# Attention side jobs of a gated cross-attention block cut into smaller steps

## The chip, the cores and the metric

One core of a Trainium2 chip runs the whole program: TensorE (matmul), VectorE, ScalarE, GpSimd and SyncE, with 16 DMA engines. The metric is device time in microseconds of one execution; lower is better.

## What is computed

The reference, cut to what matters:

```python
def xattn(f, txt):                       # f = layernorm(x): 2 x 2048 rows of 512; txt: 2 x 77 x 512
    txt_proj = txt @ Ws
    feat_proj = f @ W
    h = tanh(txt_proj[:, None] + feat_proj[:, :, None] + b)    # 2 x 2048 x 77 x 512
    rho = einsum('bftd,d->bft', h, w) + (1 - q_mask) * NEG
    att = softmax(rho, axis=-1)
    txt_h = att @ txt
    return tanh(txt_h @ Wcw + bcw) * f + tanh(txt_h @ Wcb + bcb)

def ffn(x):                              # 512 -> 1408 -> 512
    xq = fake_quant(layernorm(x))        # rounded to 127 levels of its largest magnitude
    h = fake_quant(silu(xq @ q(w_gate).T) * (xq @ q(w_up).T))
    return h @ q(w_down).T               # q: each weight row rounded to 127 levels

x = x + tanh(g_xattn) * xattn(layernorm(x), ctx)
x = x + tanh(g_ffn) * ffn(x)
```

## The kernel before

The attention is a pipeline over 924 *pieces*. A piece is one text token t and one block e of 128 features: its columns are rows of x. Pieces 0 to 307 (stage 0, 4 x 77) take the 2048 rows of batch 0, 308 to 615 (stage 1, from `PER_B`) the first 1536 rows of batch 1, 616 to 923 (stage 2, from `LAST`) its last 512. For each piece VectorE adds a column of `atxt` to the projected features `feat` and writes the sum into a ring (`add_text`, line 681); ScalarE takes the tanh in place (line 491); TensorE multiplies by the vector w and collects the scores in PSUM (`score`, line 1024, in stage 2 line 1029). ScalarE works on *units* of 6144 columns: 3 pieces in stage 0 (numbered 0 to 102), 4 in stage 1, 12 in stage 2. The ring has room for three units, so VectorE may write a piece only when TensorE has scored the one whose place it takes (`free_at`): about 9 pieces back in stage 0, 12 in stage 1, 36 in stage 2.

Each engine runs through the pieces in a loop of its own in program order, and dictionaries from piece number to job hang *side jobs* into the loops, ahead of that piece's own work. The order within a piece is that of the loop's `if`s. The names end in `_AT`; `later(at)` is `at + 10` up to piece 295 and `at + 13` after it, the piece at which VectorE fetches what TensorE made at `at`. The side jobs:

- *Projections* (`FEATS`, `FEAT_AT`, `project`, line 971): 32 blocks of 128 features by 512 rows, four matmuls each into a PSUM bank; the first four are made ahead of the loop. Phase ph (77 pieces) needs the blocks of its own e; `turns` lists at which piece of the phase before TensorE makes them. VectorE copies each block to `feat` (`copy_feat`, line 581).
- *Rows of batch 1*: statistics (`STATS_AT`, line 616), a chain of 18 small instructions (`CHAIN_AT`), then for 16 tiles normalise (`NORM_AT`, line 624), row maximum (`MAX1_AT`, line 629), transposes on TensorE (line 961), and `copy_xnT` (`COPY_AT`, line 687), which overwrites the rows of batch 0 in `xnT` and therefore waits with `dve.wait_ge(projected, Q4 * EC)` (line 686) for all 16 projections of batch 0. `MAX0_AT` holds the row maxima of batch 0.
- *Weight blocks* (`JOBS`, `QUANT_AT`): 15 blocks of the feed-forward weights (11 of 1024 columns, 4 of 1408), each reduced, scaled and rounded by VectorE (`quantise_weights`, lines 764 to 779), transposed by TensorE (`WT_AT`, line 1058) and copied out (`WCOPY_AT`). SyncE loads the next block when one is rounded.
- *Softmax*: scores are fetched (`RHO_AT`), transposed in four parts (`TSCORE_AT`, line 1042), shifted by their maximum (`SHIFT_AT`, lines 707 and 709), exponentiated by ScalarE (`EXP_AFTER`) and summed (`SUMS_AT`, `soft_sums`, lines 718 to 727).

The feed-forward part follows after the attention.

Of the kernel before, what the change touches and what calls it, by code (L numbers as in the profile page):

```python
# [5 lines left out]
def flamingo_gated_block(nc, x, ctx_in, q_mask, g_xattn, g_ffn, Ws, W, w, b, Wcw, bcw, Wcb, bcb,  # L6
# [44 lines left out]
    Q4 = 4  # L51
# [9 lines left out]
    with stack:  # L61
# [106 lines left out]
        TB, FB, WB, AB, SOFTB = (3, 4), (5, 6), (7, 4), (2, 7, 7, 7), (3, 4, 5, 6)  # L168
# [103 lines left out]
        MAX0_AT = {12 + 2 * i: i for i in range(BT)}  # L272
# [4 lines left out]
        CHAIN_AT = 150  # L277
        NORM_AT = {172 + 7 * i: i for i in range(BT)}
# [4 lines left out]
        for ph in range(B * EC):  # L283
            turns = {3: (2, 4, 14, 16), 4: (14, 16, 30, 58), 5: (30, 32, 46, 48)}.get(ph, (24, 26, 38, 40))
            for part in range(Q4 if ph < EC + 2 else Q4 - 1):
                if ph:
                    FEAT_AT[(ph - 1) * T + turns[part]] = len(FEATS)
                FEATS.append((ph // EC, ph % EC, part, ph % 2, part * 512))
        for k in range(2):
            FEAT_AT[(B * EC - 1) * T + 24 + 2 * k] = len(FEATS)  # L290
            FEATS.append((1, 2 + k, Q4 - 1, 0, k * 512))
        LAST_FEAT = ((0, 3 * 512), (1, 3 * 512), (0, 0), (0, 512))
        FEAT_COPY_AT = {later(at): f for at, f in FEAT_AT.items()}
# [20 lines left out]
        MSTD_AT, SD_AT = 530, 545  # L314
# [8 lines left out]
        def _(sp):  # L323
# [26 lines left out]
            for p in range(PIECES):  # L350
                if p in STATS_AT:
                    i = STATS_AT[p]
                    sp.wait_ge(stats_ready, BT + i + 1)
                    x_again(i + 4)
                if p in MAX1_AT and MAX1_AT[p] + 4 < BT:
                    i = MAX1_AT[p]
                    sp.wait_ge(max_ready, i + 1)
                    sp.wait_ge(xn_transposed, BT + i + 1)
                    x_again(i + 4)
                if p in QUANT_AT and QUANT_AT[p] + 1 < NJOB:  # L360
                    sp.wait_ge(wq_ready, QUANT_AT[p] + 1)
                    weight_in(QUANT_AT[p] + 1)

# [206 lines left out]
        def _(dve):  # L570
# [178 lines left out]
            def quantise_weights(job):  # L749
# [3 lines left out]
                step = width // parts  # L753
                whole = wstage[:, 0:width]
                dve.wait_ge(wt_in, sum(WT_BYTES[:job + 1]))

                def scaled():
                    for c in range(parts):
                        part = wstage[:, c * step:(c + 1) * step]
                        last = v.tensor_scalar(part, part, wsc[:, 2 + c:3 + c], MAGIC, ALU.mult, ALU.add)  # L760
                    return last

                for k, op in enumerate((
                        lambda: v.tensor_reduce(wsc[:, 0:parts], whole.rearrange("p (c d) -> p c d", c=parts), AX,  # L764
                                                ALU.max, apply_absolute_value=True),
                        lambda: v.tensor_scalar(wsc[:, 0:parts], wsc[:, 0:parts], 1.0 / QMAX, None, ALU.mult),
                        lambda: v.reciprocal(wsc[:, 2:2 + parts], wsc[:, 0:parts]),
                        scaled)):
                    if k:
                        dve.wait_ge(wt_step, lead + k)  # L770
                    op().then_inc(wt_step, 1)
                dve.wait_ge(wt_step, lead + 4)
                if job:
                    dve.wait_ge(wq_transposed, job)
                v.tensor_scalar(wq_sb[:, 0:width], whole, MAGIC, QMAX, ALU.subtract, ALU.min).then_inc(wq_ready, 1)
                if kind == "d":
                    move(sd[:, row:row + 1], wsc[:, 0:1])
                else:
                    move(sgu[:, row, :], wsc[:, 0:2])
# [12 lines left out]
            for p in range(EARLY, PIECES):  # L792
# [16 lines left out]
                if p == CHAIN_AT:  # L809
                    block_stats(BT, BT, 3)  # L810
# [9 lines left out]
                if p in FEAT_COPY_AT:  # L820
                    copy_feat(FEAT_COPY_AT[p])
                if p in WCOPY_AT:
                    copy_weights(WCOPY_AT[p])
                if p in QUANT_AT:
                    quantise_weights(QUANT_AT[p])
# [127 lines left out]
        def _(pe):  # L953
# [10 lines left out]
            def project(n):  # L964

                bt, e, part, _, _ = FEATS[n]
                pe.wait_ge(xnT_ready, BT * bt + 4 * (part + 1))
                if n >= 2:
                    pe.wait_ge(feat_ready, n - 1)
                for k in range(EC):  # L970
                    last = mm(bank(FB[n % 2]), w_sb[:, k, e * P:(e + 1) * P], xnT[:, k, part * 512:(part + 1) * 512],  # L971
                              start=(k == 0), stop=(k == EC - 1))
                last.then_inc(projected, 1)
# [72 lines left out]
            def transpose_weights(job):  # L1046
                kind, _ = JOBS[job]
                pe.wait_ge(wq_ready, job + 1)
                if job:
                    pe.wait_ge(wq_copied, job)  # L1050
                else:
                    pe.wait_ge(atxt_ready, EC)
# [4 lines left out]
                for bk, col, src in chunks:  # L1057
                    last = nc.tensor.transpose(bankb(WB[bk])[:, col:col + P], wq_sb[:, src:src + P], identb[:, :])
                last.then_inc(wq_transposed, 1)

            for p in range(PIECES):
# [17 lines left out]
                if p in FEAT_AT:  # L1079
                    n = FEAT_AT[p]  # L1080
                    if FEATS[n][:3] == (1, 1, 0):
                        pe.wait_ge(shifted, Q4)
                    project(n)
                if p in WT_AT:
                    transpose_weights(WT_AT[p])
# [114 lines left out]
```

## Time and profile before

| | us |
|---|---|
| median of 3 runs | 1412.11 |
| lowest, highest | 1405.0, 1412.8 |
| the profiled execution, its own time | 1408.1 |
| span of its profile, first to last instruction | 1406.3 |

| engine | busy us | share of the span |
|---|---|---|
| TensorE, matmul | 1110.7 | 79% |
| VectorE | 1168.8 | 83% |
| ScalarE | 1260.0 | 90% |
| GpSimd | 13.9 | 1% |

The pieces run from about 50 to 1140 us. In the rows, PE is TensorE, PEld its weight loads, DVE VectorE, ACT ScalarE; L491 is line 491. An entry in brackets is idle time of the engine ahead of that row, and who ended it. Matmuls of fp32 appear as two records each, and four column groups of scoring run side by side.

### The profile page before, as it was taken

The page shows a single profiled execution, that of the slowest core. Times are in us where ns is not written, and L with a number is a line of the kernel's source. Part 1 is how long each engine was busy: PE and PEld are TensorE (multiplying, and loading weights), DVE is VectorE, ACT ScalarE, POOL GpSimd, SP SyncE. Part 2 cuts the span into 40 slices and gives each one's busy share as a digit, 9 for nine tenths or more (in the row PEclk, how much of TensorE's full clock was granted, in tenths as well). Part 3 has the DMA queues.
Part 4 walks back from the last instruction along what each step waited for, and adds up shares of the span by engine and source line. Part 5 has one row for each costly group of instructions (what it writes and reads, how often), then busy time and mean ns, then how long its engine had stood idle before and what let it go on. Part 6 is the DMA issues. An engine that isn't in the chain of part 4 may idle for free.

```text
span 1406.3 us, 16785 instructions
## 1 busy us (share of the span) xinstructions
PE 1110.7 (79%) x6891; PEld 369.2 (26%) x6891; DVE 1168.8 (83%) x1679; ACT 1260.0 (90%) x481; POOL 13.9 (1%) x32
## 2 busy tenths in 40 slices
PE   6887768778767776679779779787667659999898
PEld 4322112212212221123222122121111115444343
DVE  7688898887899898788978878868899947888777
ACT  3998999899999999999999999999999966666695
POOL 3000000000000000000000000000000000000000
PEclk9998889889998998999999999999998879999999
DMA  6000011100010000000000010000000004411196
GB/s 219 1 15 16 16 45 60 53 23 1 23 38 32 22 24 0 1 1 6 31 21 6 16 43 1 1 0 0 1 1 0 1 16 142 150 52 48 64 346 211
DMA packets 29872, 61.43 MB, mean 44 GB/s; under 512 B 3771, under 2 KB 5835, under 8 KB 29797
## 3 DMA queue, kind: packets, MB, share of 16 engines
q1 hardware_dynamic: 27840, 59.52, 12.7%
q8 instruction: 54, 0.88, 0.3%
q10 hardware_dynamic: 1253, 0.85, 0.2%
q14 instruction: 21, 0.17, 0.0%
q0 software_dynamic: 704, 0.01, 0.0%
HBM read 46.20 MB, written 14.16 MB: 43 GB/s over the span
## 4 chain that ended last, share of the span: by engine, by line
ACT 59%; PE 27%; DVE 13%; issue 1%; DMA 0%; SPq 0%; DVEq 0%
ACT big L491 58%; PE ps L1151 10%; DVE big L681 8%; PE ps L1169 6%; PE ps L971 5%; PE ps L1024 3%; PE ps L1029 1%; DVE bn L616 1%; PE ps L1117 1%; PE ps L1131 0%; DMA wgu<-in_x_dram 0%; DVE big L581 0%; DVE wsc L764 0%; DVE wgu L624 0%; PE ps L961 0%
## 5 line engine op out<-in xcount | busy, mean ns | idle before, releaser
L491 ACT ACTIVATE big<-big 128x6144 f32<-128x6144 f32 (+2 forms) x205 | 1063.6, 5279 | 21.4 <-DVE big L681 21.3
L681 DVE TENSOR_SCALAR big<-big,atxt 128x2048 f32<-128x2048 f32 (+2 forms) x918 | 792.8, 922 | 154.6 <-PE ps L1024 139.5
L1024 PE MATMUL ps<-big,wslide 128*32 128x512 f32 x4312 | 615.1, 643 | 215.3 <-ACT big L491 212.0
L1024 PEld LDWEIGHTS ps<-big,wslide 128*32 128x32 f32 x4312 | 143.3, 114 | 645.0 <-ACT big L491 335.4
L1151 PE MATMUL ps<-aux,wgu 128*128 128x512 bf16 x680 | 151.5, 379 | 0.0
L1029 PE MATMUL ps<-big,wslide 128*32 128x512 f32 x616 | 91.1, 700 | 43.4 <-ACT big L491 43.4
L971 PE MATMUL ps<-big,aux 128*128 128x512 f32 x256 | 118.3, 605 | 2.1 <-ACT big L449 2.1
L536 ACT ACTIVATE aux<-ps,sgux 128x512 f32<-128x512 f32 x88 | 59.9, 686 | 56.8 <-PE ps L1151 55.9
L916 DVE SCALAR_TENSOR_TENSOR big<-ps,sgux,aux 128x512 f32<-128x512 f32 x88 | 65.9, 749 | 25.3 <-PE ps L1151 17.0
L1151 PEld LDWEIGHTS ps<-aux,wgu 128*128 128x128 bf16 x680 | 65.3, 98 | 73.4
L1169 PE MATMUL ps<-wd,wgu 128*128 128x512 bf16 x352 | 78.1, 386 | 3.0 <-DVE wgu L932 3.0
L971 PEld LDWEIGHTS ps<-big,aux 128*128 128x128 f32 x256 | 46.2, 190 | 73.1 <-issue 69.4
L919 DVE TENSOR_REDUCE hm<-big 128x1 f32<-128x512 f32 x88 | 60.4, 686 | 3.0
L1029 PEld LDWEIGHTS ps<-big,wslide 128*32 128x32 f32 x616 | 21.3, 123 | 109.4 <-ACT big L491 63.2
L549 ACT ACTIVATE big<-big,gmax 128x1408 int16<-128x1408 f32 x32 | 46.1, 1453 | 3.5 <-DVE gmax L882 3.5
L1169 PEld LDWEIGHTS ps<-wd,wgu 128*128 128x128 bf16 x352 | 34.8, 99 | 46.0 <-issue 5.7
L946 DVE TENSOR_TENSOR aux<-ps,aux 128x512 f32<-128x512 f32 x32 | 21.9, 685 | 16.7 <-DMA out_dram<-aux 8.9
L511 ACT ACTIVATE aux<-aux,beta,alpha 128x512 int16<-128x512 f32 x32 | 25.8, 809 | 9.4 <-DVE sgux L891 5.2
L557 ACT ACTIVATE aux<-aux,resB,resA 128x512 f32<-128x512 f32 x32 | 25.7, 802 | 6.1 <-DVE aux L949 4.6
L449 ACT ACTIVATE big<-ps 128x512 f32<-128x512 f32 x16 | 8.9, 596 | 17.2 <-PE ps L961 17.2
L949 DVE TENSOR_TENSOR aux<-aux 128x512 f32<-128x512 f32 x32 | 22.1, 692 | 1.1
L519 ACT ACTIVATE aux<-ps 128x512 bf16<-128x512 bf16 x32 | 18.9, 591 | 4.1 <-PE ps L1117 4.1
(153 smaller groups left out, 419.3 us busy)
## 6 DMA issues: line engine op xcount, KB each, us to landing
aux<-in_x_dram SPq DMA_DIRECT2D x96, 256.0 KB, 2.7
out_dram<-aux SPq DMA_DIRECT2D x32, 256.0 KB, 3.6
hidden_spill<-big SPq DMA_DIRECT2D x6, 768.0 KB, 5.5
big<-hidden_spill SPq DMA_DIRECT2D x6, 768.0 KB, 7.3
wgu<-in_x_dram SPq DMA_DIRECT2D x11, 256.0 KB, 7.3
aux<-in_L_ffn_w_gate_dram SPq DMA_DIRECT2D x11, 256.0 KB, 2.6
aux<-in_L_ffn_w_up_dram SPq DMA_DIRECT2D x11, 256.0 KB, 2.9
aux<-in_L_ffn_w_down_dram SPq DMA_DIRECT2D x4, 704.0 KB, 4.0
```

Source lines behind the costliest of these rows:

```text
L491: nc.scalar.activation(unit, unit, ACT.Tanh).then_inc(tanh_done, 1)
L511: nc.scalar.activation(xu[:, n % 2, :], xt[:, n % 3, :], ACT.Identity, bias=beta[:, n:n + 1], scale=alpha[:, n:n + 1]).then_inc(xu_ready, 1)
L536: nc.scalar.activation(sg[:, m % 2, :], bank(m % 3), ACT.Silu, scale=sgux[:, i, 0:1])\
L549: nc.scalar.activation(h_int[:, slot2[q], :, j, 0:P], part, ACT.Copy, scale=gmax[:, 3:4]).then_inc(hu_ready, 1)
L681: v.tensor_scalar(ring[:, place(p)], src, atxt[:, e, bt * T + t:bt * T + t + 1], None, ALU.add).then_inc(sums_ready, 1)
L916: v.scalar_tensor_tensor(h_slots[:, rb % SLOTS, i, :], bank(3 + m % 3), sgux[:, i, 1:2], sg[:, m % 2, :], ALU.mult, ALU.mult).then_inc(h_r ...
L919: v.tensor_reduce(hm[:, m:m + 1], h_slots[:, rb % SLOTS, i, :], AX, ALU.max, apply_absolute_value=True).then_inc(dve_step, 1)
L971: last = mm(bank(FB[n % 2]), w_sb[:, k, e * P:(e + 1) * P], xnT[:, k, part * 512:(part + 1) * 512], start=(k == 0), stop=(k == EC - 1))
L1024: last = mm(bank(k)[32 * part:32 * part + 32, :], wslide[:, e, 31 - g:63 - g], unit[:, part * 512:(part + 1) * 512], start=(e == 0 and g = ...
L1029: last = mm(bank(LB)[32 * j:32 * j + 32, :], wslide[:, e, 31 - g:63 - g], unit, start=(e == 0 and g == 0), stop=True, skip_group_check=True)
L1151: last = mm(bank(3 * g + m % 3), wgu8[:, 2 * k + g, i * P:(i + 1) * P], xqT[:, rb % 2, k, :], start=(k == 0), stop=(k == EC - 1))
L1169: last = mm(bank(n % 6), hq[:, q % 2, i, j * P:(j + 1) * P], wd[:, i, :], start=(i == 0), stop=(i == IC - 1))
```

## The change

Projections become four single matmuls, at the piece given by `turns` and two, four and six pieces later, and `turns` itself is set anew; TensorE's waits stand at the first, the signal at the last. Weight blocks become four steps of VectorE in successive pieces, at new pieces (`JOB_AT`), and their transposes two halves. The chain of 18 becomes three parts of six. The rows of batch 1 start at piece 164, every 6 pieces, instead of 172, every 7; row maxima of batch 0 stand every 4 pieces instead of 2. Score transposes, shifts and sums are spread wider, the sums of batch 0 ten pieces apart instead of four, and the score transposes use banks 3 and 4 only, so parts 2 and 3 wait for parts 0 and 1 to be shifted. Two waits of VectorE on its own earlier work are added: at the start of a chain, and ahead of the first copy of a phase's features.

```diff
-        TB, FB, WB, AB, SOFTB = (3, 4), (5, 6), (7, 4), (2, 7, 7, 7), (3, 4, 5, 6)
+        TB, FB, WB, AB, SOFTB = (3, 4), (5, 6), (7, 4), (2, 7, 7, 7), (3, 4, 3, 4)
...
-        MAX0_AT = {12 + 2 * i: i for i in range(BT)}
+        MAX0_AT = {12 + 4 * i: i for i in range(BT)}
...
-        CHAIN_AT = 150
-        NORM_AT = {172 + 7 * i: i for i in range(BT)}
+        CHAIN_AT = {148 + 2 * k: k for k in range(3)}
+        NORM_AT = {164 + 6 * i: i for i in range(BT)}
         MAX1_AT = {at + 2: i for at, i in NORM_AT.items()}
         COPY_AT = {later(at): i for at, i in NORM_AT.items()}
...
-            turns = {3: (2, 4, 14, 16), 4: (14, 16, 30, 58), 5: (30, 32, 46, 48)}.get(ph, (24, 26, 38, 40))
+            turns = {3: (-17, -9, 2, 10), 5: (20, 30, 40, 50)}.get(ph, (10, 20, 30, 40))
             for part in range(Q4 if ph < EC + 2 else Q4 - 1):
                 if ph:
-                    FEAT_AT[(ph - 1) * T + turns[part]] = len(FEATS)
+                    for k in range(EC):
+                        FEAT_AT[(ph - 1) * T + turns[part] + 2 * k] = len(FEATS), k
...
-            FEAT_AT[(B * EC - 1) * T + 24 + 2 * k] = len(FEATS)
+            for i in range(EC):
+                FEAT_AT[(B * EC - 1) * T + 10 + 12 * k + 2 * i] = len(FEATS), i
...
-        FEAT_COPY_AT = {later(at): f for at, f in FEAT_AT.items()}
+        FEAT_COPY_AT = {max(later(at), T * (FEATS[f][1] - 1)): f
+                        for at, (f, k) in FEAT_AT.items() if k == EC - 1}
...
-        QUANT_AT = dict(zip((50, 64, 80, 96, 112, 128, 200, 220, 262, 365, 378, 400, 445, 475, 522), range(NJOB)))
-        WT_AT = {at + 1: j for at, j in QUANT_AT.items()}
-        WCOPY_AT = {later(at + 1): j for at, j in QUANT_AT.items()}
+        JOB_AT = (59, 75, 91, 107, 123, 179, 204, 229, 262, 276, 290, 400, 430, 460, 490)
+        QUANT_AT = {at + k: (job, k) for job, at in enumerate(JOB_AT) for k in range(4)}
+        WT_AT = {at + 4 + h: (job, h) for job, at in enumerate(JOB_AT) for h in range(2)}
+        WCOPY_AT = {later(at + 5): job for job, at in enumerate(JOB_AT)}
...
-        TSCORE_AT = {PER_B + 1 + c: (0, c) for c in range(Q4)}
-        TSCORE_AT.update({LAST + 42 + 2 * c: (1, c) for c in range(Q4)})
-        SHIFT_AT = {PER_B + 16 + 4 * c: (0, c) for c in range(Q4)}
-        SHIFT_AT.update({LAST + 84 + 24 * c: (1, c) for c in range(Q4)})
-        EXP_AFTER = {UNIT_OF[at] + 2: f for at, f in SHIFT_AT.items()}
-        SUMS_AT = {at + (24 if at < LAST else 72): f for at, f in SHIFT_AT.items()}
+        TSCORE_AT = {PER_B + at: (0, c) for c, at in enumerate((3, 6, 34, 40))}
+        TSCORE_AT.update({LAST + at: (1, c) for c, at in enumerate((42, 48, 100, 112))})
+        SHIFT_AT = {PER_B + at: (0, c) for c, at in enumerate((20, 26, 48, 54))}
+        SHIFT_AT.update({LAST + at: (1, c) for c, at in enumerate((84, 96, 140, 152))})
+        EXP_AFTER = {UNIT_OF[at] + 1: f for at, f in SHIFT_AT.items()}
+        SUMS_AT = {PER_B + at: (0, c) for c, at in enumerate((62, 72, 82, 92))}
+        SUMS_AT.update({LAST + at: (1, c) for c, at in enumerate((180, 204, 228, 252))})
...
-        MSTD_AT, SD_AT = 530, 545
+        MSTD_AT, SD_AT = 520, 530
...
-                if p in QUANT_AT and QUANT_AT[p] + 1 < NJOB:
-                    sp.wait_ge(wq_ready, QUANT_AT[p] + 1)
-                    weight_in(QUANT_AT[p] + 1)
+                if p in QUANT_AT and QUANT_AT[p][1] == 3 and QUANT_AT[p][0] + 1 < NJOB:
+                    sp.wait_ge(wq_ready, QUANT_AT[p][0] + 1)
+                    weight_in(QUANT_AT[p][0] + 1)
...
-                    if k:
+                    if lead + k:
                         dve.wait_ge(dve_chain, lead + k)
...
-                if p == CHAIN_AT:
-                    block_stats(BT, BT, 3)
+                if p in CHAIN_AT:
+                    k = CHAIN_AT[p]
+                    dve.wait_ge(stats_ready, TILES)
+                    chained(STAT * 3 + 6 * k, mean_rstd_ops(slice(BT, TILES))[6 * k:6 * k + 6])
...
                 if p in FEAT_COPY_AT:
+                    if FEATS[FEAT_COPY_AT[p]][2] == 0 and p > T:
+                        dve.wait_ge(sums_ready, T * (p // T) - EARLY)
                     copy_feat(FEAT_COPY_AT[p])
...
-            def project(n):
+            def project(n, steps=range(EC)):
...
-                pe.wait_ge(xnT_ready, BT * bt + 4 * (part + 1))
-                if n >= 2:
-                    pe.wait_ge(feat_ready, n - 1)
-                for k in range(EC):
+                if 0 in steps:
+                    pe.wait_ge(xnT_ready, BT * bt + 4 * (part + 1))
+                    if n >= 2:
+                        pe.wait_ge(feat_ready, n - 1)
+                for k in steps:
...
-                last.then_inc(projected, 1)
+                if EC - 1 in steps:
+                    last.then_inc(projected, 1)
...
             def transpose_scores(bt, c):
+                if c >= 2:
+                    pe.wait_ge(shifted, Q4 * bt + c - 1)
```

Left out here are the body of `quantise_weights`, which does the same instructions in steps 0 (reduction), 1 (scale and reciprocal), 2 (scaling) and 3 (rounding, signal), and that of `transpose_weights`, cut into the first four chunks and the rest. A wait of TensorE for `shifted`, ahead of the first projection of phase 5, falls away with the new banks.

## Rows read from the trace of the kernel before

**Rows 1.** The page, part 1: busy us, share of the span, instructions.

```profile
PE 1110.7 (79%) x6891; PEld 369.2 (26%) x6891; DVE 1168.8 (83%) x1679; ACT 1260.0 (90%) x481; POOL 13.9 (1%) x32
```

**Rows 2.** Waits, whole span: who waited for whom, us, times, longest us.

```profile
PE ps L1024 <- ACT big L491: 212.0, 130, 6.3
DVE big L681 <- PE ps L1024: 139.5, 119, 3.6
ACT big L491 <- DVE big L681: 21.3, 15, 4.5
```

**Rows 3.** Waits from 53 to 330, to 600, to 690, to 1023, to 1141 us.

```profile
ACT big L491 <- DVE big L681: 11.0, 5, 4.5
...
ACT big L491 <- DVE big L681: 1.3, 1, 1.3
...
ACT big L491 <- DVE big L681: 3.6, 3, 2.2
...
ACT big L491 <- DVE big L681: 3.7, 3, 1.9
...
ACT big L491 <- DVE big L681: 1.8, 3, 0.8
```

**Rows 4.** Chain that ended last, two stretches: start us, us, what.

```profile
116.01 3.75 PE ps L971 x8
...
121.61 3.63 PE ps L971 x8
...
128.19 1.14 DVE wsc L764
...
132.67 94.00 ACT big L491 x18
...
638.92 1.85 PE ps L1024 x12
```

**Rows 5.** Timeline, ScalarE, TensorE, VectorE in stage 0: start us, us, what, idle before.

```profile
273.26 234.79 ACT L491 ACTIVATE big<-big 128x6144 f32<-128x6144 f32 x45 [3.79 <-DVE big L681]
...
325.58 2.78 PE L1024 MATMUL ps<-big,wslide 128*32 128x512 f32 x24 [0.73 <-ACT big L491]
...
326.71 3.68 DVE L681 TENSOR_SCALAR big<-big,atxt 128x2048 f32<-128x2048 f32 x3 [0.51 <-PE ps L1024]
...
349.16 1.13 PE L971 MATMUL ps<-big,aux 128*128 128x512 f32 x2
...
440.31 3.52 PE L1024 MATMUL ps<-big,wslide 128*32 128x512 f32 x16 [2.44 <-ACT big L491]
443.76 0.70 PE L961 MATMUL ps<-ident,aux 128*128 128x128 f32 x4
```

**Rows 6.** Timeline, VectorE: row jobs of stage 0, a sum and a weight block.

```profile
453.94 0.54 DVE L624 TENSOR_SCALAR aux<-aux,mean,rstd 128x512 f32<-128x512 f32 x1
...
458.59 0.68 DVE L687 COPY big<-ps 128x512 f32<-128x512 f32 x1
...
649.77 0.95 DVE L718 TENSOR_TENSOR aux<-big,crow 128x768 f32<-128x768 f32 x1
...
652.16 3.80 DVE L681 TENSOR_SCALAR big<-big,atxt 128x1536 f32<-128x1536 f32 x4
...
662.91 1.21 DVE L764 TENSOR_REDUCE wsc<-aux 128x2 f32<-128x1024 f32 x1
...
666.15 1.94 DVE L681 TENSOR_SCALAR big<-big,atxt 128x1536 f32<-128x1536 f32 x2
```

**Rows 7.** Windows: us, busy by engine, granted clock of PE, DMA share, GB/s.

```profile
140.00:310.00 170.00, 126.01 (x844) 32.74 (x840) 148.89 (x173) 165.27 (x33) 0.00 (x0) 0.87 0.13 41
680.00:1013.00 333.00, 260.25 (x1633) 70.89 (x1633) 272.38 (x340) 329.32 (x65) 0.00 (x0) 1.00 0.03 12
```

**Rows 8.** Timeline, VectorE in stage 2: a sum and 24 additions.

```profile
1086.86 0.75 DVE L718 TENSOR_TENSOR aux<-big,crow 128x576 f32<-128x576 f32 x1
...
1088.75 9.58 DVE L681 TENSOR_SCALAR big<-big,atxt 128x512 f32<-128x512 f32 x24
```

More of the change, by code:

```diff
@@ L747, in soft_last, with quantise_weights @@
                 v.tensor_reduce(num[:, :, TILES - Q4:TILES], prod_last, AX, ALU.add).then_inc(soft_step, 1)
-            def quantise_weights(job):
+            def quantise_weights(job, step):
                 kind, row = JOBS[job]
@@ L752, in quantise_weights @@
                 lead = 4 * job
-                step = width // parts
+                part = width // parts
                 whole = wstage[:, 0:width]
-                dve.wait_ge(wt_in, sum(WT_BYTES[:job + 1]))
-                def scaled():
-                    for c in range(parts):
[L759 to L777, printed above, removed]
-                else:
-                    move(sgu[:, row, :], wsc[:, 0:2])
+                if step == 0:
+                    dve.wait_ge(wt_in, sum(WT_BYTES[:job + 1]))
+                    v.tensor_reduce(wsc[:, 0:parts], whole.rearrange("p (c d) -> p c d", c=parts), AX,
+                                    ALU.max, apply_absolute_value=True).then_inc(wt_step, 1)
+                elif step == 1:
+                    dve.wait_ge(wt_step, lead + 1)
+                    v.tensor_scalar(wsc[:, 0:parts], wsc[:, 0:parts], 1.0 / QMAX, None, ALU.mult).then_inc(wt_step, 1)
+                    dve.wait_ge(wt_step, lead + 2)
+                    v.reciprocal(wsc[:, 2:2 + parts], wsc[:, 0:parts]).then_inc(wt_step, 1)
+                elif step == 2:
+                    dve.wait_ge(wt_step, lead + 3)
+                    for c in range(parts):
+                        row_part = wstage[:, c * part:(c + 1) * part]
+                        last = v.tensor_scalar(row_part, row_part, wsc[:, 2 + c:3 + c], MAGIC, ALU.mult, ALU.add)
+                    last.then_inc(wt_step, 1)
+                else:
+                    dve.wait_ge(wt_step, lead + 4)
+                    if job:
+                        dve.wait_ge(wq_transposed, job)
+                    v.tensor_scalar(wq_sb[:, 0:width], whole, MAGIC, QMAX, ALU.subtract, ALU.min).then_inc(wq_ready, 1)
+                    if kind == "d":
+                        move(sd[:, row:row + 1], wsc[:, 0:1])
+                    else:
+                        move(sgu[:, row, :], wsc[:, 0:2])
@@ L824, in _ @@
                 if p in QUANT_AT:
-                    quantise_weights(QUANT_AT[p])
+                    quantise_weights(*QUANT_AT[p])
                 if p in RHO_AT:
@@ L962, in transpose_rows @@
                 last.then_inc(xn_transposed, 1)
-            def project(n):
+            def project(n, steps=range(EC)):
                 bt, e, part, _, _ = FEATS[n]
-                pe.wait_ge(xnT_ready, BT * bt + 4 * (part + 1))
-                if n >= 2:
-                    pe.wait_ge(feat_ready, n - 1)
-                for k in range(EC):
+                if 0 in steps:
[3 more added lines that the diff above has]
+                for k in steps:
                     last = mm(bank(FB[n % 2]), w_sb[:, k, e * P:(e + 1) * P], xnT[:, k, part * 512:(part + 1) * 512],
-                              start=(k == 0), stop=(k == EC - 1))
-                last.then_inc(projected, 1)
+                              start=(k == 0), stop=(k == EC - 1), skip_group_check=True)
+                if EC - 1 in steps:
+                    last.then_inc(projected, 1)
             def project_text(e):
@@ L1044, in transpose_scores, with transpose_weights @@
                 last.then_inc(rho_transposed, 1)
-            def transpose_weights(job):
+            def transpose_weights(job, half):
                 kind, _ = JOBS[job]
[L1048 to L1052, printed above, removed]
+                if half == 0:
+                    pe.wait_ge(wq_ready, job + 1)
+                    if job:
+                        pe.wait_ge(wq_copied, job)
+                    else:
+                        pe.wait_ge(atxt_ready, EC)
                 if kind == "d":
@@ L1056, in transpose_weights @@
                     chunks = [(0, (2 * k + g) * P, g * D + k * P) for k in range(EC) for g in range(2)]
-                for bk, col, src in chunks:
+                for bk, col, src in chunks[4:] if half else chunks[:4]:
                     last = nc.tensor.transpose(bankb(WB[bk])[:, col:col + P], wq_sb[:, src:src + P], identb[:, :])
-                last.then_inc(wq_transposed, 1)
+                if half:
+                    last.then_inc(wq_transposed, 1)
             for p in range(PIECES):
@@ L1079, in _ @@
                 if p in FEAT_AT:
[L1080 to L1083, printed above, removed]
+                    n, k = FEAT_AT[p]
+                    project(n, (k,))
                 if p in WT_AT:
-                    transpose_weights(WT_AT[p])
+                    transpose_weights(*WT_AT[p])
                 if p == SD_AT + 1:
```

## The prediction

> **What bounds the kernel now.** I read the page's engine line first, then the waits, the chain, and the timeline around the longest waits. ScalarE is the busiest engine, 1260.0 us of the 1406.3 [rows 1]. In the attention it does little but the tanh over units of 6144 columns; 45 of them in a row took 234.79 us, 5.22 us each [rows 5]. The first question is therefore how long ScalarE waits there: 21.3 us, in 15 waits, every time for VectorE's additions (line 681) [rows 2]. That is all a rearrangement of side jobs can give back. The same waits by stretch show where: 11.0 us up to 330, 1.3 up to 600, 3.6 around 650, 3.7 up to 1023 and 1.8 after it [rows 3].
>
> The chain tells why. Before the longest wait (4.5 us [rows 2], ending at 132.67 [rows 4]) TensorE runs two whole projections, 3.75 and 3.63 us, with two pieces between them; scoring is late, VectorE gets its ring slots late, then meets a weight block at 128.19, and ScalarE runs dry [rows 4]. A weight block holds VectorE from 662.91 to 666.15, 3.24 us; a softmax sum from 649.77 to 652.16, 2.4 us [rows 6].
>
> How much lateness is free? In a clean stretch TensorE starts scoring a unit at 325.58; VectorE follows with three additions from 326.71 and is done at 330.39, 4.8 us after 325.58 [rows 5]. Those additions are read two tanhs after that scoring starts, 10.4 us. So up to about 5.6 us of lateness costs nothing, and what is over is ScalarE's wait. Per piece VectorE has free time of 5.22/3 - 1.2 = 0.54 us in stage 0 (three additions in 3.68 us less the overlap [rows 5]) and 5.22/4 - 0.93 = 0.37 in stage 1 (four in 3.80 [rows 6]). As a test: from piece 348 to 365 the old schedule has sums at 348, 352, 356 and 360, copies at 351, 353 and a weight block at 365: with the copies 4 x 2.4 + 1.3 + 3.2 = 14.1 us against 17 x 0.37 = 6.3 free, 7.8 over; less 5.6 leaves 2.2, and the two projections at 354 and 356 make it worse; the trace has 3.6 [rows 3]. The rule is good to a microsecond or so.
>
> **The change, part by part.**
>
> *Projections.* 28 blocks of 3.63 us become 112 single matmuls, one every second piece. What does a single one cost TensorE? A quarter of 3.63 is 0.91, the lower bound, if coming and going between line 1024 and line 971 costs nothing. A row that ends after the first matmul of a projection (two records of line 971) has 1.13 for it [rows 5], the upper bound, with its own start and end. I take 1.1, as each now stands alone. In stage 0 a unit then has 2.78 us of scoring [rows 5] plus at most 2 x 1.1: 5.0, under 5.22. In stage 1 ten pieces have 10 x 0.92 (two pieces 1.85 [rows 4]) + 4 x 1.1 = 13.6 against 10 x 1.305 = 13.05: 0.55 late for each projection, some 2 us over the four from piece 328 on, and with the score transposes in the same stretch about 3 to 4. That stays inside 5.6. So the projections' waits go.
>
> The Trainium skill (TensorEngine Tiling (Array Packing), Overview, Key Properties) speaks against this part: changing the tiling mode, not just the tile, drains TensorE. Scoring runs on 128*32 and the projection on 128*128, so the changes of mode rise from 56 to 224. The trace agrees in kind: 1.13 for one against 0.91 for a quarter of four [rows 4, 5]. The page has no price for it; with the drain at 1.13 as without it at 0.91 the sum is the same, as both stay inside the free lateness, and only far more would move it (second rival).
>
> *Softmax.* The sums stand ten pieces apart instead of four: 2.4 against 10 x 0.37 = 3.7 free. The 3.6 us around 650 go. At piece 400 the last sum meets the first step of a weight block of 1408 columns: 2.4 + at most 4.5 (3.24 x 1408/1024) in four pieces, 3.7 of additions: 10.6 us where 5.2 + 5.6 = 10.8 are to be had. It just fits; I put 0.3 there.
>
> *Weight blocks in steps and the statistics chain in three.* The same instructions, so VectorE's sum is unchanged; each dip is shared among four pieces. The new waits of VectorE on its own earlier instruction (chain start, the part-0 copies) have what they wait for many pieces behind them, but at piece 154, where it is the instruction before: nothing to 0.2 us. SyncE issues the next block's two loads at the fourth step instead of the only one, 11 or more pieces (19 us) ahead of their use, behind waits that VectorE meets in the same order: hidden.
>
> *Stage 2.* VectorE needs 9.58 us for 24 additions [rows 8] where ScalarE has 10.44: 0.45 us free per unit. A sum takes 1.9 [rows 8]. Before, shifts and sums from 700 to 844 (4 x 1.9, and 4 x 0.9, estimated as half a sum, 11 us) ran against some 12 units x 0.45; now to 868, with the score transposes on TensorE set apart. I count the 1.8 us [rows 3] as gone, with nothing to 1.8 as bounds.
>
> *A new wait.* The second batch's rows move from piece 172 on to 164 on, and the copy that overwrites xnT with the first of them from 182 to 174. That copy waits for all 16 projections of batch 0 (line 686). The last is still not done before piece 170 on TensorE. VectorE can run some 9 pieces ahead of TensorE's scoring in stage 0; 182 was 12 pieces behind 170 and never met that wait, 174 is 4 behind and must. Everything queued behind it on VectorE waits too, the additions first. Let E be the end of tanh for pieces 168-170. TensorE then scores 168 and 169 (2 x 0.93), transposes rows at 170 (0.70 [rows 5]) and does the last matmul (1.1): E + 3.65. VectorE: copy 0.6 (0.68 with its overlap), additions 174 and 175 of 1.2 each, normalise 0.5 [rows 6], addition 176 of 1.28: E + 8.4. ScalarE, done with 171-173, wants it at E + 5.2: 3.2 us idle. The lead is now zero, so what comes next costs in full: pieces 177-179 with a row maximum 0.6 and the weight block's 1.2 reduction make 5.4 against 5.2, idle 0.2; 180-182 with two copies (1.2), the other 2.0 of the block, a normalise 0.5 and 3.6 of additions make 7.3, idle 2.1. Together 5.5 us. From below: 3 us if the block is better hidden than that; from above 8.5 if TensorE is at its lower clock then, since two pieces there took 3.52 instead of 1.85 [rows 5] and a matmul stretches alike.
>
> *Sum.* 21.3 - 5.5 - 0.3 - 0.4 for small dips = 15.1 us. The profiled execution took 1408.1, so 1393.0. The three timed runs have a median of 1412.1, 0.3% above that execution; the same 15.1 from it gives **1397 us**, a ratio of 0.989.
>
> **Rivals.**
>
> *All of it comes back.* The wait at 174 finds VectorE late anyway, or TensorE earlier than I reckon. For it: VectorE waited 139.5 us for scoring in all, and little of that reached ScalarE [rows 2]. Against it: TensorE's order at 170 is fixed. Then 21.3 - 0.5: 1412.1 - 20.8 = 1391.
>
> *TensorE cannot carry the single matmuls in stage 1, and the wait at 174 is dearer.* At 1.5 us each, ten pieces need 15.2 against 13.05, 2.1 late per projection: the four from 328 make 8.6 and are 3 over the 5.6; the others of stage 1 stand in groups of two or three and stay near it. With 8.5 at 174: 21.3 - 8.5 - 3 - 1 = 9, 1403. For it: 1.13 is one row, and no row has a lone matmul between scorings. Against: TensorE waited 212.0 us for ScalarE [rows 2], and 84 more comings and goings at 0.2 are 17.
>
> *Slower: TensorE's clock.* With its bursts of two projections gone, TensorE might stay at 1.2 GHz for long. At that level two pieces took 3.52 [rows 5], 5.3 a unit, just over a tanh, before any side job. From 140 to 310 the granted clock is 0.87, so about a quarter of that time is already at the lower level, and the slow scoring at 440.31 came after TensorE had waited 2.44 us for ScalarE [rows 5]; from 680 to 1013 it is 1.00 [rows 7]. If it stayed low through stage 0's 103 units, scoring (5.3) and the 64 single matmuls there at 2.2 (1.4 a unit) would make 6.7 a unit against 5.2: 103 x 1.5 = 155 us more. It decides from 29 us of that, about a fifth: 15 for the gain and 14 beyond, 1426 and up. Against it: single matmuls stand in the gaps after which the clock fell.
>
> The Trainium skill (TensorE: Matmul & The Clock Gate, section HAM oscillation) sides with this rival: short bursts with idle between them let the clock drop again and again, and it advises doing the matmuls in one go ahead of a wait. Here two in one go preceded ScalarE's longest wait [rows 4]; what the rule would do is in the 155 us above.
>
> **How the numbers follow.** The forecast (12 to 19 us gained) 0.48; all back 0.15; half lost (4 to 12 gained) 0.31; slower 0.06. A measurement of this kernel can tell about 1% from no change, 14.1 us. Faster by over 1%: the second, 0.15, and some 0.34 of the first, as 14.1 lies a third of the way up its 12 to 19: 0.49. Within 1%: 0.14 + 0.31 = 0.45. Slower 0.06. The range reaches from 1388, all back in a run of the faster kind, to 1408, where 4 us are gained; the forecast alone is 1393 to 1400.
>
> **What would show it.** Right: ScalarE's waits for line 681 fall from 21.3 to 5-8 us, and the longest are two or three close together near 340 us, behind a VectorE copy of line 687's kind that waits for TensorE's projection; no wait remains near 130, 270, 660 and 745; line 971 costs TensorE about 1.1 per matmul. Wrong: waits between 630 and 760 with TensorE never idle (second rival), a granted clock well under 0.87 between 140 and 310 (third), or no long VectorE wait near 340 (first).

## The result, and the profile after

The changed kernel's median is 1389.0 us (1387.7 to 1392.0), against 1409.6 for the kernel before (four runs of each): a ratio of 0.9875, 95% interval 0.9853 to 0.9897. That is 20.6 us faster, where 15 were forecast; the time lies inside the range, close to its lower end. It is 8 us under the 1397 of the forecast: 5.5 of them are the larger gain, and 2.5 the kernel before, whose median was 1412.1 in three runs and is 1409.6 in four.

| | before | after |
|---|---|---|
| profiled execution, us | 1408.1 | 1387.7 |
| its span | 1406.3 | 1385.9 |
| ScalarE's waits for the additions | 21.3 in 15 | 5.0 in 3 |

The page, part 1, of the changed kernel (busy us, share of the span, instructions; compare [rows 1]):

```profile
PE 1114.8 (80%) x6868; PEld 348.3 (25%) x6891; DVE 1167.7 (84%) x1679; ACT 1258.5 (91%) x481; POOL 13.9 (1%) x32
```

VectorE and ScalarE work as long as before to 0.2%, and TensorE's matmuls a little longer; only the span is shorter. In the changed kernel line 681 is 687 (additions), 491 is 497 (tanh), 1024 is 1035 (scoring), 971 is 981 (projection), 686 and 687 are 692 and 693 (copy to `xnT`). Its waits, whole span (us, times, longest; compare [rows 2]):

```profile
PE ps L1035 <- ACT big L497: 186.9, 137, 5.6
...
DVE big L687 <- PE ps L1035: 117.0, 145, 2.7
...
DVE big L693 <- PE ps L981: 7.9, 1, 7.9
...
ACT big L497 <- DVE big L687: 5.0, 3, 3.1
```

The third line is new: one copy of VectorE that waits 7.9 us for a projection. The timeline of ScalarE shows what is left of its waits (start us, us, what, idle before; compare [rows 3, 5]):

```profile
51.46 292.14 ACT L497 ACTIVATE big<-big 128x6144 f32<-128x6144 f32 x56
346.68 10.63 ACT L497 ACTIVATE big<-big 128x6144 f32<-128x6144 f32 x2 [3.09 <-DVE big L687]
358.95 259.19 ACT L497 ACTIVATE big<-big 128x6144 f32<-128x6144 f32 x50 [1.64 <-DVE big L687]
...
1096.12 24.57 ACT L497 ACTIVATE big<-big 128x6144 f32<-128x6144 f32 x6 [0.26 <-DVE big L687]
1124.57 0.47 ACT L501 ACTIVATE big<-big 128x320 f32<-128x320 f32 x1 [3.88 <-DVE big L743]
```

Fifty-six tanhs run without a gap from 51.46, where the old kernel had waits up to 4.5 us; then come two waits, 3.09 and 1.64, and one of 0.26 in stage 2. VectorE's timeline around the two:

```profile
332.73 1.28 DVE L687 TENSOR_SCALAR big<-big,atxt 128x2048 f32<-128x2048 f32 x1
341.91 0.69 DVE L693 COPY big<-ps 128x512 f32<-128x512 f32 x1 [7.90 <-PE ps L981]
342.52 2.47 DVE L687 TENSOR_SCALAR big<-big,atxt 128x2048 f32<-128x2048 f32 x2
344.91 0.55 DVE L630 TENSOR_SCALAR aux<-aux,mean,rstd 128x512 f32<-128x512 f32 x1
345.37 2.48 DVE L687 TENSOR_SCALAR big<-big,atxt 128x2048 f32<-128x2048 f32 x2
...
349.55 1.21 DVE L763 TENSOR_REDUCE wsc<-aux 128x2 f32<-128x1024 f32 x1
```

The copy stands at piece 174, the two additions are 174 and 175, normalise and addition 176 follow, and 346.68 is when ScalarE gets them. TensorE's timeline has the other side, the last matmul of projection 15 at piece 170, behind the transposes of a row tile:

```profile
338.44 1.92 PE L1035 MATMUL ps<-big,wslide 128*32 128x512 f32 x16 [0.18 <-ACT big L497]
340.29 0.66 PE L970 MATMUL ps<-ident,aux 128*128 128x128 f32 x4
340.78 1.02 PE L981 MATMUL ps<-big,aux 128*128 128x512 f32 x2
```

From 338.44 the forecast counted 3.65 us to the end of that matmul; the copy starts 3.47 after it.

Where do the 20.4 us of span come from? From the start of the first tanh to the end of the last one it is 1069.2 us instead of 1087.1, 17.9 less. ScalarE's waits give 16.3 of that. Each wait also costs the overlap of two tanhs: 45 in a row run 5.22 us apart [rows 5] while one alone lasts 5.33 (the row at 549.57 further down is such a one); twelve waits fewer are some 1.2 us. Outside that stretch, the first tanh starts at 51.46 instead of 52.85 (1.4), the last exponential waits 3.88 instead of 5.41 (1.5), and 0.4 are lost after it. That 1.4 and 1.5 are the change's is not shown: among the nine experiments below, the first tanh starts between 51.6 and 56.2, and the last wait is 3.9 in three and 5.3 to 5.4 in six, where kernels that are alike at that end have either value. It goes with the length of the last 40 records of scoring on TensorE: 4.66 us in the four traces with the short wait, 6.1 to 6.2 in the other seven. The granted clock in them is 1.00 here and 0.72 before (windows of those records).

### The profile page after: what moved, and what is told of

Its sections match the earlier page's. It is cut to its first block, busy times and chain, and to the rows that moved or that the text cites. A ratio compares the mean times of both kernels' runs of the same rounds, so it can differ in the third digit from the quotient of the medians.

```text
span 1385.9 us, 16773 instructions
## 1 busy us (share of the span) xinstructions
PE 1114.8 (80%) x6868; PEld 348.3 (25%) x6891; DVE 1167.7 (84%) x1679; ACT 1258.5 (91%) x481; POOL 13.9 (1%) x32
## 4 chain that ended last, share of the span: by engine, by line
ACT 72%; PE 19%; DVE 8%; issue 1%; DMA 0%; SPq 0%; DVEq 0%
ACT big L497 71%; PE ps L1164 11%; PE ps L1182 6%; DVE big L687 4%; DVE bn L622 1%; PE ps L981 1%; PE ps L1130 1%; PE ps L1144 0%; DMA wgu<-in_x_dram 0%; PE ps L1040 0%; DVE wgu L630 0%; ACT big L469 0%; ACT big L455 0%; DVE block_sums L730 0%; DVE aux L724 0%
## 5 line engine op out<-in xcount | busy, mean ns | idle before, releaser
L1035 PEld LDWEIGHTS ps<-big,wslide 128*32 128x32 f32 x4312 | 131.4, 112 | 611.4 <-ACT big L497 322.6
L981 PE MATMUL ps<-big,aux 128*128 128x512 f32 x256 | 140.3, 638 | 2.1 <-ACT big L455 2.1
L981 PEld LDWEIGHTS ps<-big,aux 128*128 128x128 f32 x256 | 39.1, 188 | 99.1 <-issue 95.4
L1040 PEld LDWEIGHTS ps<-big,wslide 128*32 128x32 f32 x616 | 20.0, 120 | 108.0 <-ACT big L497 65.9
```

The lines of the kernel that those rows point to most:

```text
L1035: last = mm(bank(k)[32 * part:32 * part + 32, :], wslide[:, e, 31 - g:63 - g], unit[:, part * 512:(part + 1) * 512], start=(e == 0 and g = ...
L1040: last = mm(bank(LB)[32 * j:32 * j + 32, :], wslide[:, e, 31 - g:63 - g], unit, start=(e == 0 and g == 0), stop=True, skip_group_check=True)
```

## Experiments

Theory: ScalarE waits only for lateness beyond VectorE's lead, the 5 to 6 us by which its additions are ready before ScalarE wants them. So the gain is owed to where the jobs stand, not to how small they are, and the 5 us left are the wait of piece 174. The rivals: the cutting itself brought the gain; the weight block at 179 causes the waits that are left. Ratios are to the kernel before, run on the same chip; intervals are 95%. Most of these intervals overlap one another, so the differences between the kernels rest on the waits in one trace of each and on the stretch from the first tanh's start to the last one's end there, which leaves out the scatter of the beginning and the end.

| kernel | median us | ratio | interval | ScalarE's waits, us | first to last tanh, us |
|---|---|---|---|---|---|
| before | 1409.6 | 1 | | 21.3 | 1087.1 |
| changed | 1389.0 | 0.9875 | 0.9853 to 0.9897 | 5.0 | 1069.2 |
| rows from 170 | 1384.5 | 0.9843 | 0.9816 to 0.9870 | none | 1063.8 |
| rows from 170, whole projections | 1386.5 | 0.9857 | 0.9825 to 0.9889 | 0.6 | 1065.4 |
| rows from 170, whole weight blocks | 1386.1 | 0.9849 | 0.9834 to 0.9863 | 1.4 | 1065.4 |
| rows from 170, close sums | 1384.9 | 0.9849 | 0.9815 to 0.9882 | 0.8 | 1065.1 |
| rows from 170, all three in one go | 1393.7 | 0.9893 | 0.9871 to 0.9915 | 6.9 | 1072.1 |
| changed, weight block 5 at 190 | 1386.8 | 0.9857 | 0.9820 to 0.9895 | 3.1 | 1067.1 |
| before, new places for projections alone | 1392.2 | 0.9892 | 0.9876 to 0.9908 | 5.3 | 1069.9 |
| before, cut projections alone | 1399.1 | 0.9932 | 0.9906 to 0.9957 | 13.2 | 1078.9 |
| rows from 170, a dose of lateness (one run) | 1384.5 | | | 0.3 | 1064.4 |

**Rows from piece 170.**

```diff
-        NORM_AT = {164 + 6 * i: i for i in range(BT)}
+        NORM_AT = {170 + 6 * i: i for i in range(BT)}
```

> The changed kernel with one edit: the rows of batch 1 start at piece 170 instead of 164, so the copy that waits for all 16 projections stands at piece 180, ten behind the last projection matmul at 170. Theory (the wait at 174 caused both waits of ScalarE, 3.09 and 1.64 us): both vanish, ScalarE's waits fall from 5.0 to under 1 us, time about 5 us below the changed kernel, ratio to the kernel before about 0.984. Rival (the weight block at 179 to 182 meeting the row jobs is the cause): a wait of 1.5 us or more stays within pieces 180 to 188, gain at most 3 us.

Measured: 1384.5 us, 4.5 less than the changed kernel's median; from the first tanh to the last it is 5.4 less. ScalarE's timeline has 108 tanhs without a gap, to the first exponential of the softmax, and VectorE's first copy to `xnT`, now at piece 180, waits for nothing:

```profile
53.96 561.69 ACT L497 ACTIVATE big<-big 128x6144 f32<-128x6144 f32 x108
```

```profile
347.42 0.68 DVE L693 COPY big<-ps 128x512 f32<-128x512 f32 x1
```

Both waits are gone with the weight block where it was, so it was the wait at 174. By its waits this kernel is better than the changed one; the intervals of their two ratios overlap.

**Weight block 5 at 190.**

```diff
-        JOB_AT = (59, 75, 91, 107, 123, 179, 204, 229, 262, 276, 290, 400, 430, 460, 490)
+        JOB_AT = (59, 75, 91, 107, 123, 190, 204, 229, 262, 276, 290, 400, 430, 460, 490)
```

> The changed kernel with the rows from 164 as it has them, but weight block 5 at pieces 190 to 193 instead of 179 to 182. Theory: the first wait (3.1 us at unit 58) stays, the second (1.64 us at unit 60) goes or falls under 0.4; 1.3 to 1.7 us gained on the changed kernel. Rival (the block is the cause of both): both go, 4.7 us.

The first wait stays to the hundredth, the second is gone; VectorE still waits 7.9 us at its copy (timeline of ScalarE, then the waits):

```profile
347.47 269.62 ACT L497 ACTIVATE big<-big 128x6144 f32<-128x6144 f32 x52 [3.09 <-DVE big L687]
```

```profile
DVE big L693 <- PE ps L981: 7.9, 1, 7.9
```

The wait at 174 takes the lead, and the block that stands next then costs ScalarE 1.64 us. The rival of the block falls.

**Whole projections, new places.** On the first experiment:

```diff
                     n, k = FEAT_AT[p]
-                    project(n, (k,))
+                    if k == EC - 1:
+                        project(n)
```

> The first experiment's kernel (rows from 170), but each projection is again four matmuls in one go, at the piece of its last single matmul; the pieces ten apart stay. Theory of free lateness (5.3 to 5.6 us; a block of 3.63 us makes TensorE that late once and it catches up before the next): ScalarE's waits stay under 1.5 us, time within 2 us of the first experiment. Rival (it is the cutting into single matmuls that removed the waits): the waits of the kernel before come back at the projections, 8 us or more.

Measured: 0.6 us of waits, all that its timeline of ScalarE has:

```profile
98.86 386.34 ACT L497 ACTIVATE big<-big 128x6144 f32<-128x6144 f32 x74 [0.25 <-DVE big L687]
485.36 129.04 ACT L497 ACTIVATE big<-big 128x6144 f32<-128x6144 f32 x25 [0.15 <-DVE big L687]
...
1092.35 24.57 ACT L497 ACTIVATE big<-big 128x6144 f32<-128x6144 f32 x6 [0.20 <-DVE big L687]
```

Its median is 2.0 us over the first experiment's; the last exponential's wait alone differs by 1.5 in the profiles (5.40 against 3.88), and it falls either way. At ten pieces apart the cutting is worth 0.6 us of waits.

**Whole weight blocks.** On the first experiment, all four steps at the block's first piece:

```diff
-                    quantise_weights(*QUANT_AT[p])
+                    if QUANT_AT[p][1] == 0:
+                        for step in range(4):
+                            quantise_weights(QUANT_AT[p][0], step)
```

> The first experiment's kernel (rows from 170), but each weight block is rounded in one go at its first piece, as before. Theory: a block of 3.2 to 4.4 us in one piece is inside the free lateness; the lead was least (0.13 us) at the block of pieces 430 to 433, so 0 to 2 us of ScalarE's waits in all. Rival (the steps removed waits): 3 us or more.

Measured: two waits, 1.03 at piece 430's block, as expected of the place with the least lead, and 0.36 in stage 2, where no weight block stands. Timelines of VectorE and ScalarE:

```profile
730.89 1.61 DVE L763 TENSOR_REDUCE wsc<-aux 128x1 f32<-128x1408 f32 x1
...
734.78 3.80 DVE L687 TENSOR_SCALAR big<-big,atxt 128x1536 f32<-128x1536 f32 x4
```

```profile
736.76 292.27 ACT L497 ACTIVATE big<-big 128x6144 f32<-128x6144 f32 x56 [1.03 <-DVE big L687]
```

**Close sums.** On the first experiment:

```diff
-        SUMS_AT = {PER_B + at: (0, c) for c, at in enumerate((62, 72, 82, 92))}
+        SUMS_AT = {PER_B + at: (0, c) for c, at in enumerate((62, 66, 70, 74))}
```

> The first experiment's kernel, but the four softmax sums of batch 0 stand four pieces apart (370, 374, 378, 382) instead of ten, as before. Theory: 4 x 2.4 us and a copy of 0.6 against 12 x 0.37 free is 5.8 over; the lead of VectorE at piece 364 was 2.7 us in the changed kernel, so about 3 us (2 to 4) of ScalarE's waits near 670 to 690 us. Rival (the sums cost nothing without pairs of projections): no wait there.

Measured: one wait of 0.78 us, where 2 to 4 were expected; the rival, no wait, is nearly as good. I had set the sums against the free time of 12 pieces; they lie in four units, 16 pieces with 6 us, which leaves 10.2 - 6.0 - 2.7 = 1.5. Timeline of ScalarE:

```profile
673.63 354.87 ACT L497 ACTIVATE big<-big 128x6144 f32<-128x6144 f32 x68 [0.78 <-DVE big L687]
```

The softmax sums alone, then, do not cost the 3.6 us of [rows 3]: those were sums, a weight block and a pair of projections together (see the new places alone, below).

**All three in one go.** The three edits above on the first experiment.

> The first experiment's kernel with projections and weight blocks in one go and the sums four pieces apart: only the places of the jobs are new. Theory (places, not step size, gave the time): ScalarE's waits 2 to 6 us, time still 14 us or more below the kernel before. Rival (step size gave it): waits of 15 us or more, most of the gain gone.

Measured: 6.9 us in ten waits, a little over the 2 to 6 expected. Its median is 9.2 us over the first experiment's, which ran on another chip (8.3 from the first tanh to the last), and 13.5 below the kernel before on the same chip (1407.3), where 14 or more were expected. The rival, 15 us of waits or more, falls. The parts alone cost 0.6, 1.4 and 0.8, 2.8 together. The same lead covers each of them, and not their sum. The longest wait, timeline of TensorE, VectorE and ScalarE:

```profile
532.21 1.21 PE L1037 MATMUL ps<-big,wslide 128*32 128x512 f32 x8 [2.44 <-ACT big L497]
533.35 5.21 PE L983 MATMUL ps<-big,aux 128*128 128x512 f32 x8
...
539.62 1.29 DVE L687 TENSOR_SCALAR big<-big,atxt 128x2048 f32<-128x2048 f32 x1 [4.87 <-PE ps L1037]
...
545.00 1.21 DVE L763 TENSOR_REDUCE wsc<-aux 128x2 f32<-128x1024 f32 x1
...
549.57 5.33 ACT L497 ACTIVATE big<-big 128x6144 f32<-128x6144 f32 x1 [1.49 <-DVE big L687]
```

A whole projection takes the lead, and a whole weight block follows before VectorE has it back. The projection takes 5.21 us here instead of 3.7: the granted clock in it is 0.71 (window 533.35 to 538.56), after TensorE had waited 2.44 us for ScalarE. So a part of this wait is likely TensorE's clock and not the places; no run separates the two.

**New places alone.** On the kernel before; everything but the projections' places is as it was:

```diff
-            turns = {3: (2, 4, 14, 16), 4: (14, 16, 30, 58), 5: (30, 32, 46, 48)}.get(ph, (24, 26, 38, 40))
+            turns = {3: (2, 8, 12, 18), 4: (14, 24, 34, 58), 5: (30, 40, 50, 60)}.get(ph, (16, 26, 36, 46))
...
-            FEAT_AT[(B * EC - 1) * T + 24 + 2 * k] = len(FEATS)
+            FEAT_AT[(B * EC - 1) * T + 16 + 10 * k] = len(FEATS)
```

> The kernel before with one edit: its whole projections stand 6 to 14 pieces apart (mostly 10) instead of in pairs two pieces apart; weight blocks, rows, softmax as before. Theory: the waits at the pairs go (12.2 us up to 600, 3.7 us from 690 to 1023); 3 to 6 us of 21.3 are left around the softmax and in stage 2; time 15 to 18 us below the kernel before, ratio 0.987 to 0.990. Rival (a whole projection is too large a step anywhere): 10 us or more of the waits left.

Measured: 15.1 us below the kernel before on the same chip, 5.3 us of waits left, both as expected: 2.02 at 267, 0.83 and 1.63 near 660, 0.35 at 724, 0.45 in stage 2. Near 660 ScalarE's timeline has:

```profile
653.97 5.33 ACT L491 ACTIVATE big<-big 128x6144 f32<-128x6144 f32 x1 [0.83 <-DVE big L681]
660.94 62.73 ACT L491 ACTIVATE big<-big 128x6144 f32<-128x6144 f32 x12 [1.63 <-DVE big L681]
```

Two lines of places take away 16.0 of the 21.3 us of waits. By the medians that is three quarters of the gain; from the first tanh to the last it is 17.2 of 17.9, and the intervals of the two ratios overlap. What all the other edits of the change can be worth in waits is about the 5.3 left here, and the rows moved to 164 give 4.7 back at piece 174. The statistics chain in three parts, the row maxima and the new banks were not tried alone.

**Cuts alone.** On the kernel before, projections as single matmuls from where the pairs stood, the second of a pair in the pieces between (phase 3 left whole):

```diff
-                    FEAT_AT[(ph - 1) * T + turns[part]] = len(FEATS)
+                    at = (ph - 1) * T + turns[part]
+                    pair = part % 2 and turns[part] - turns[part - 1] == 2
+                    for k in range(EC) if ph != 3 else (EC - 1,):
+                        FEAT_AT[at - pair + 2 * k if ph != 3 else at] = len(FEATS), k
...
```

Left out here: the same for the last two blocks, the places of the copies, and `project` in steps, as in the change.

> The kernel before with one edit: its projections (but those of phase 3) are single matmuls two pieces apart, started where the whole blocks stood; the second of a pair runs in the pieces between. Places of all other jobs as before. Theory (only lateness over about 5.3 us counts; a single costs TensorE 1.19 us by the changed kernel's trace): in stage 0 eight pieces then need 8 x (0.91 + 1.19) = 16.8 us against 13.9, 2.9 late, so its 12.2 us of waits fall under 1.5; in stage 1 16.8 against 10.4, 6.4 late, so the waits from 690 to 1023 stay, 3 to 5 us, as do those near 650 (3 to 5) and in stage 2 (about 1.8). In all 9 to 12 of 21.3 left, 10 to 13 us gained. Rival A (only place counts): 18 or more left. Rival B (small steps suffice anywhere): under 6 left.

Measured: 8.9 us faster, 13.2 us of waits left in 13, a little over the 9 to 12 expected. In stage 0 11.2 of 12.3 us are gone: cutting is there another way of spreading. From 690 to 1023 the five waits make 6.2 us, more than the old 3.7; three of them:

```profile
737.33 26.39 ACT L495 ACTIVATE big<-big 128x6144 f32<-128x6144 f32 x5 [0.91 <-DVE big L685]
765.35 78.39 ACT L495 ACTIVATE big<-big 128x6144 f32<-128x6144 f32 x15 [1.62 <-DVE big L685]
844.78 20.97 ACT L495 ACTIVATE big<-big 128x6144 f32<-128x6144 f32 x4 [1.04 <-DVE big L685]
```

Each of these follows a pair or a weight block behind one. Of a pair's eight matmuls one stands behind every piece, and TensorE's timeline has 2.05 us for a piece and a matmul together, from 721.83 to 723.88; VectorE's has the block:

```profile
721.83 1.13 PE L976 MATMUL ps<-big,aux 128*128 128x512 f32 x2
722.89 1.06 PE L1030 MATMUL ps<-big,wslide 128*32 128x512 f32 x6
723.88 1.13 PE L976 MATMUL ps<-big,aux 128*128 128x512 f32 x2
```

```profile
758.54 1.61 DVE L768 TENSOR_REDUCE wsc<-aux 128x1 f32<-128x1408 f32 x1
```

Eight such are 16.4 us against 10.4, 6.0 late and so 0.7 over a lead of 5.3; the three pairs of this stretch cost 0.91, 1.04 and 0.97. Two whole projections with two pieces between them are 3.63 + 1.85 + 3.63 = 9.1 us against 2.6 [rows 4], 6.5 late: in stage 1 the cutting hardly changes that. After two of the pairs a third projection and a weight block follow before the lead is back, and cost 1.62 and 1.61. So the five waits follow the same account, and the two blocks are what the expectation left out; its 16.8 us for eight pieces were near, though a single matmul takes 1.06 and not 1.19, and a piece between two of them 0.99 and not 0.91. Both rivals fall: neither the place alone nor the small step alone is "the" cause, spreading is, and in stage 1 places do it better.

**A dose of lateness.** On the first experiment, matmuls that nobody reads:

```diff
+        DOSE = {444: (4, 27), 520: (6, 30), 588: (8, 32)}
...
+                if p in DOSE:
+                    pe.wait_ge(feat_ready, DOSE[p][1])
+                    for _ in range(DOSE[p][0]):
+                        mm(bank(FB[0]), w_sb[:, 0, 0:P], xnT[:, 0, 0:512], start=True, stop=True, skip_group_check=True)
```

> The first experiment's kernel with extra matmuls on TensorE, whose results nobody reads, at three quiet places of stage 1: 4 in a row at piece 444 (about 3.7 us), 6 at 520 (5.5 us), 8 at 588 (7.3 us). It measures the free lateness. Theory (5.3 us, the lead of VectorE in these places): ScalarE's waits 0 at the first, 0 to 0.5 at the second, 2.0 (1.5 to 2.5) at the third. Rival (any lateness of TensorE costs ScalarE): 3.7, 5.5 and 7.3.

Measured, in one run: no wait at any of the three; 2.0 us were expected at the last. Timelines of TensorE and of VectorE there:

```profile
938.57 3.63 PE L1036 MATMUL ps<-big,wslide 128*32 128x512 f32 x24 [1.59 <-ACT big L498]
943.78 3.63 PE L1036 MATMUL ps<-big,wslide 128*32 128x512 f32 x24 [1.58 <-ACT big L498]
947.35 7.13 PE L1098 MATMUL ps<-big,aux 128*128 128x512 f32 x16
954.41 10.98 PE L1036 MATMUL ps<-big,wslide 128*32 128x512 f32 x75
```

```profile
944.90 3.81 DVE L688 TENSOR_SCALAR big<-big,atxt 128x1536 f32<-128x1536 f32 x4 [1.40 <-PE ps L1036]
955.53 11.25 DVE L688 TENSOR_SCALAR big<-big,atxt 128x1536 f32<-128x1536 f32 x12 [6.82 <-PE ps L1036]
```

The eight fill the 1.58 us in which TensorE would have waited anyway; scoring starts at 954.41 where one unit after 943.78 would be 948.99, so TensorE is 5.4 us late. VectorE waits 6.82 us instead of 1.40 and is done with its first four additions at 959.34; ScalarE takes them at 959.37, having lost only the overlap of 0.2 us. So some 5.3 us of lateness are free here, as worked out, and a burst that begins in TensorE's idle time may be 1.6 longer.

## Why the prediction was right, point by point

**Free lateness.** Right: 5.6 forecast from [rows 5] for stage 0, 5.3 measured by dose in stage 1; stage 0 had no dose. The miss in that experiment was to leave out TensorE's own idle time.

**The new wait at 174.** Right in place, cause and size: 3.2, 0.2 and 2.1 us forecast for units 58, 59 and 60; 3.09, none and 1.64 measured, 4.7 for 5.5 together. The 7.9 us that VectorE waits show that it came with its whole lead, as forecast.

**The projections' waits go.** Right, but the prediction did not say which part of the edit does it. Places alone take away 16.0 us of waits, cuts alone 8.1, and with the places new the cuts are worth 0.6. What a single matmul costs was chosen well, 1.1 between 0.91 and 1.13. Timeline of TensorE in the changed kernel:

```profile
815.76 1.92 PE L1035 MATMUL ps<-big,wslide 128*32 128x512 f32 x12
817.61 1.12 PE L981 MATMUL ps<-big,aux 128*128 128x512 f32 x2
818.66 1.92 PE L1035 MATMUL ps<-big,wslide 128*32 128x512 f32 x12
820.51 1.12 PE L981 MATMUL ps<-big,aux 128*128 128x512 f32 x2
...
824.47 3.63 PE L1035 MATMUL ps<-big,wslide 128*32 128x512 f32 x24
828.03 1.13 PE L981 MATMUL ps<-big,aux 128*128 128x512 f32 x2
```

From start to start one matmul is 817.61 to 818.66, 1.05, and four in a row are 3.63 [rows 4], each with one coming and one going between 128*32 and 128*128: so a matmul itself is 0.86, and coming and going cost 0.19 in that row. The 1.13 that the prediction set against 0.91 is the length of two records up to their modelled end, and does not show this. Scoring pays too: two pieces are 1.85 and four 3.56 (824.47 to 828.03), so two are 1.71 and 0.14 are for the change. That makes 0.33 us for one coming and going, and 84 more are 28 us of TensorE, more than the prediction's 17, none of which reached ScalarE. The Trainium skill (TensorEngine Tiling (Array Packing), Overview, Key Properties) says that a change of mode drains TensorE. The trace agrees in that every change costs; how much of the 0.33 is the drain it does not show.

**Softmax, weight blocks, stage 2.** The waits went as forecast (the 0.26 at 1096 is what is left of 1.8). But the paragraph on the softmax lets the 3.6 us near 650 go because of the sums alone, and close sums cost 0.8 by themselves. The prediction's own test had it better: sums, copies and the weight block 2.2, and the pair of projections on top. With the pair apart and the rest as before, the places alone left 0.83 and 1.63 there, 2.5.

**The sum.** 6.2 us of waits forecast, 5.0 found: 1.2 too dear, 0.8 at piece 174 and 0.4 for piece 400 and small dips. The other 4.1 of the 5.3 by which the profiled execution beat the forecast are some 1.2 of overlap, which the prediction did not count, and 2.9 at the beginning and the end, which it had no term for. No run shows those to be the change's, so that they fell this way is luck.

**Rivals.** All back: not so, as 5.0 us stayed, though the gain of 20.6 us lies nearer to that rival's 20.8 than to the forecast's 12 to 19; the waits tell the two apart, the time does not. TensorE too slow in stage 1: no, 1.05 and not 1.5 each. Slower by the clock: the granted clock from 140 to 310 rose from 0.87 [rows 7] to 0.94 (windows of the changed kernel; columns as there):

```profile
140.00:310.00 170.00, 131.49 (x872) 30.59 (x876) 152.91 (x176) 170.00 (x34) 0.00 (x0) 0.94 0.14 41
680.00:1000.00 320.00, 259.51 (x1582) 64.69 (x1576) 266.91 (x339) 320.00 (x62) 0.00 (x0) 1.00 0.03 10
```

ScalarE is busy for the whole of both windows. From 330 to 600 the clock hardly differs (0.92 before, 0.91 after). That single matmuls are what raises it is borne out by the first experiment and the one with whole projections, which differ in that alone: over the whole span the granted clock is 0.954 to 0.962 in the five runs with singles, and 0.947 to 0.953 in the four with whole projections. The Trainium skill (TensorE: Matmul & The Clock Gate, section HAM oscillation) advises doing matmuls in one go ahead of a wait. Here it was the other way: single matmuls in the gaps went with a higher clock.

## What to carry to other kernels

In a pipeline with one saturated engine, work out the lead of the engine that feeds it, and set it against everything that falls within the time in which the lead comes back: a side job within it is nearly free at any step size (0.6 to 1.4 us here), and two that are free alone need not be free together. Spread jobs before cutting them. When a consumer of a side job is moved earlier, count how far its producer lies behind it in the other engine's order; at four pieces, less than the ring's nine, the wait took the whole lead here and the next job paid too; at ten it cost nothing. What lies between was not tried.

## What was not expected of the hardware

- A wait of ScalarE costs some 0.1 us more than its idle time: back-to-back tanhs start 5.22 us apart, and one alone lasts 5.33.
- Between matmuls on 128*32, one on 128*128 costs TensorE 0.33 us more than the 0.86 that it takes within a row of four, 0.19 at the matmul and 0.14 at the scoring around it.
- The last exponential waits 3.9 or 5.4 us in kernels that are alike there, by how long the last scoring takes TensorE (40 records in 4.66 us, or in 6.1 to 6.2); the first tanh starts 51.5 to 56.2 us into the span, for a reason that stays open. Both are larger than what several of these edits change, so the waits in a profile tell these kernels apart better than a median does.
